# Scores and weighted sums in halves, and the work of every step in a new order on all engines

## What is computed

```python
def attn_layer(x, Wqkv, qs, ksc, Wo):
    qkv = x @ Wqkv
    q, k, v = jnp.split(qkv, 3, -1)          # 16 heads of 64
    q = l2norm(q) * qs
    k = l2norm(k) * ksc
    q = q * cos * scale + rotate_half(q) * sin * scale
    k = k * cos * inv + rotate_half(k) * sin * inv
    out = local_attention(q, k, v)           # softmax over this window and the one before
    return out @ Wo

def ffn_layer(x, g, bln, W1, b1, W2, b2):
    xn = (x - mu) / jnp.sqrt(var + 1e-05) * g + bln
    hg = xn @ W1 + b1
    a, gate = jnp.split(hg, 2, -1)           # 341 each
    return a * jax.nn.gelu(gate, approximate=False) @ W2 + b2

for i in range(6):
    x = attn_layer(shift_tokens(x), ...) + x
    x = ffn_layer(shift_tokens(x), ...) + x
```

## Time and profile before

| | |
|---|---|
| median of 3 runs | 1618.8 us (1618.2 to 1619.11) |
| the profiled execution, its own time | 1619.38 us |
| its span in the profile | 1617.6 us |
| TensorE busy | 1544.3 us, 95% |
| weight loads | 907.8 us, 56% |
| VectorE, ScalarE, GpSimd busy | 1234.8, 1232.5, 1222.1 us, each 76% |
| instructions of TensorE | 30224 MATMUL and 30224 LDWEIGHTS |
| mean granted clock | 0.987 |

### The profile page before, as it was taken

How to read it: one execution, slowest core, us unless ns; L and a number is a source line. 1 busy time by engine, 2 the same in 40 slices (tenths; PEclk the granted TensorE clock), 3 DMA queues, 4 the chain that set the end, 5 groups by cost and what they waited for, 6 DMA issues and landing times.

```text
span 1617.6 us, 69676 instructions
## 1 busy us (share of the span) xinstructions
PE 1544.3 (95%) x30224; PEld 907.8 (56%) x30224; DVE 1234.8 (76%) x1693; ACT 1232.5 (76%) x2368; POOL 1222.1 (76%) x1051
## 2 busy tenths in 40 slices
PE   7879999999999999999999999999999999999995
PEld 6745556555555555555556555555565565555553
DVE  5488878778778778777877778778778788787873
ACT  4347787787787787887887887887887887887871
POOL 6169888777787778778777787787787787787861
PEclk9989999999999999999999999999999999999998
DMA  5000000100000100000100000100000000000000
GB/s 193 28 2 27 10 7 5 61 7 6 22 6 7 35 29 10 18 7 9 36 28 10 9 16 10 33 31 9 9 16 9 7 5 9 7 18 9 7 12 27
DMA packets 24545, 32.60 MB, mean 20 GB/s; under 512 B 2372, under 2 KB 21424, under 8 KB 23344
## 3 DMA queue, kind: packets, MB, share of 16 engines
q1 hardware_dynamic: 24240, 28.15, 5.4%
HBM read 20.80 MB, written 1.05 MB: 14 GB/s over the span
## 4 chain that ended last, share of the span: by engine, by line
PE 75%; ACT 7%; issue 5%; DVE 3%; POOL 1%; DMA 0%; ACTq 0%; SPq 0%; POOLq 0%; DVEq 0%
PE ring L274 20%; PE psq L254 18%; PE ring L262 9%; PE ring L308 8%; PE pss L292 7%; PE ring L325 4%; PE ring L318 4%; PE pss L283 2%; DVE qb L927 2%; ACT L1126 2%; ACT sq L1096 1%; ACT uT L1126 1%; ACT pr L1100 1%; ACT kT L1107 1%; PE ring L649 1%
## 5 line engine op out<-in xcount | busy, mean ns | idle before, releaser
L254 PE MATMUL psq<-wqk,x0S 128*128 128x512 f32 x768 | 379.4, 617 | 4.0 <-issue 3.1
L274 PE MATMUL ring<-mh,x0S 128*32 128x512 f32 x3072 | 369.6, 598 | 7.4 <-ACT uT L1126 7.4
L1305 POOL TENSOR_TENSOR qa<-qa,qb 128x1024 f32<-128x1024 f32 x96 | 228.9, 2384 | 63.0 <-DVE qb L848 62.9
L1361 POOL TENSOR_TENSOR pr<-pr,rden 128x1024 f32<-128x1024 f32 x96 | 183.9, 1915 | 88.3 <-DVE rden L824 88.0
L1357 POOL TENSOR_TENSOR qa<-qa,qb 128x1024 f32<-128x1024 f32 x96 | 226.7, 2361 | 0.4 <-DVE qb L927 0.3
L254 PEld LDWEIGHTS psq<-wqk,x0S 128*128 128x128 f32 x768 | 135.8, 192 | 130.0 <-issue 120.8
L308 PEld LDWEIGHTS ring<-u,pT 128*32 128x32 f32 x6144 | 172.9, 111 | 61.4 <-issue 61.4
L904 DVE TENSOR_TENSOR qa<-psq,tab 128x1024 f32<-128x1024 f32 x96 | 117.5, 1224 | 105.5 <-PE psq L254 105.5
L308 PE MATMUL ring<-u,pT 128*32 128x128 f32 x6144 | 187.0, 274 | 3.2 <-ACT pT L1228 3.2
L1323 POOL TENSOR_TENSOR qa<-qa,rn 128x1024 f32<-128x1024 f32 x96 | 182.7, 1903 | 7.5
L274 PEld LDWEIGHTS ring<-mh,x0S 128*32 128x32 f32 x3072 | 80.0, 109 | 190.5 <-issue 172.6
(11 more groups left out here) (174 smaller groups left out, 2819.8 us busy)
## 6 DMA issues: line engine op xcount, KB each, us to landing
wqk<-in_wqk SPq DMA_DIRECT2D x6, 1024.0 KB, 4.9
mvT<-in_mvT SPq DMA_DIRECT2D x6, 512.0 KB, 5.6
wo<-in_wo SPq DMA_DIRECT2D x6, 512.0 KB, 8.7
xf<-x SPq DMA_DIRECT2D x24, 128.0 KB
xf<-x SPq DMA_DIRECT2D x24, 127.0 KB
rope<-in_rope SPq DMA_DIRECT2D x1, 2048.0 KB, 10.0
w<-in_w SPq DMA_DIRECT2D x6, 341.0 KB, 3.8
xmid<-in_x SPq DMA_DIRECT2D x4, 256.0 KB, 4.0
```

Of the source, the lines that this page charges most:

```text
L254: return mm(psq[:, 512 * (n % 2):512 * (n % 2) + 512], x0S[:, tile * P:tile * P + P], wqk[:, l % 2, 512 * n:512 * n + 512], start=True, st ...
L274: last = mm(bank[WIN * g:WIN * g + WIN, :], x0S[:, tile * P + WIN * w:tile * P + WIN * w + WIN], mh[:, l % 2, g, :, :].rearrange("p j n -> ...
L1305: g_.tensor_tensor(qa[:, t % 2, 0:1024], qa[:, t % 2, 0:1024], qb[:, 0:1024], ALU.add).then_inc(sum_q, 1)
L1361: g_.tensor_tensor(p4[t % 2], p4[t % 2], rden[:, :].unsqueeze(1).unsqueeze(3).broadcast_to([P, 2, HEADS, WIN]), ALU.mult).then_inc(p_ready, 1)
```

## The change

Four edits of TensorE's work go together, with a new order and new lags on every engine:

- `scores` is called twice a tile, pairs 0 to 3 after the mask at the end of step t+3, pairs 4 to 7 in step t+4. `mix` is called twice, and the values of U0 stand between its halves.
- `project` and `hidden` get a second form, in pieces of 32 columns, which no call uses: `WHOLE_P` and `WHOLE_H` list every product as whole.
- The lags: keys and queries of tile t in step t+1, both transposes one behind the other in t+3, P in t+5, Y in t+6 (five steps behind the projections; before, three). F stands 12 steps behind the projection of its group's first tile (before, 8), Z 14 (before, 11), X 15 (before, 12). TensorE's step is now the step of the other engines, and the loop has two steps more.
- The scan's chunks 4 to 7 stand in step 0, ahead of the first projection; 8 to 11 in step 1, 12 to 15 in step 2.
- ACT, DVE and POOL are put in the matching order; the semaphores `l_bst` and `l_rs` are split in two; weight loads of the feed-forward part are issued two steps later (`LOAD_W` 9).

```diff
+WHOLE_P = [0, 1, 2, 3]
+WHOLE_H = [(0, 1), (1, 1), (2, 1), (0, 0), (1, 0), (2, 0)]
...
-            def scores(t):
-
-                for pair in range(PAIRS):
+            def scores(t, half):
+
+                for pair in range(4 * half, 4 * half + 4):
...
-            def mix(bank, t):
-
-                for b in range(4):
+            def mix(bank, t, part):
+
+                for b in (2 * part, 2 * part + 1):
...
-            for s in range(STEPS + 17):
...
+            for s in range(STEPS + 19):
...
+                t = s - 4
+                if 0 <= t < STEPS:
+                    scores(t, 1).then_inc(s_ready, 1)
...
+                    mix(ring[bank], t, 0)
...
+                    values(ring[bank], t, 0).then_inc(filled[bank], 1)
...
+                    mix(ring[bank], t, 1).then_inc(filled[bank], 1)
...
+                t = s - 3
+                if 0 <= t < STEPS:
+                    wait(pe, p_shifted, t)
+                    mask(t)
...
+                    scores(t, 0)
```

More of the change, by code:

```diff
@@ L498, in _ @@
             features(0)
-            for s in range(STEPS + 17):
-                t = s - 7
+            for s in range(STEPS + 19):
+                t = s - 6
                 if 0 <= t < STEPS:
-                    bank, n = take("U2", t)
-                    wait(pe, freed[bank], n)
-                    values(ring[bank], t, 2).then_inc(filled[bank], 1)
                     bank, n = take("U3", t)
@@ L525, in _ @@
[L525 to L534, removed]
+                u = unit_at(s, 3)
+                if u >= 0:
+                    features(u)
@@ new lines, in _ @@
+                i = group_at(s, 14)
+                if i >= 0:
+                    bank, n = take("G0", i)
+                    nbank, m = place["F", i]
+                    pe.wait_ge(freed[nbank], m + 1)
+                    if i % GROUPS == 0:
+                        pe.wait_ge(w1_ready, 16 * (i // GROUPS + 1))
+                    wait(pe, freed[bank], n)
+                    hidden(ring[bank], 0, 1).then_inc(filled[bank], 1)
+                    bank, n = take("A0", i)
+                    wait(pe, freed[bank], n)
+                    hidden(ring[bank], 0, 0).then_inc(filled[bank], 1)
@@ new lines, in _ @@
+                i = group_at(s, 15)
+                if i >= 0:
+                    bank, n = take("A1", i)
+                    wait(pe, freed[bank], n)
+                    hidden(ring[bank], 1, 0).then_inc(filled[bank], 1)
+                    bank, n = take("A2", i)
+                    wait(pe, freed[bank], n)
+                    hidden(ring[bank], 2, 0).then_inc(filled[bank], 1)
+                t = s - 5
+                if 0 <= t < STEPS:
+                    bank, n = take("U1", t)
+                    wait(pe, freed[bank], n)
+                    values(ring[bank], t, 1).then_inc(filled[bank], 1)
@@ new lines, in _ @@
+                if i >= 0:
+                    act.wait_ge(nmr_ready, i + 1)
+                    if i > 0:
+                        abank, m = place["A2", i - 1]
+                        act.wait_ge(filled[abank], m + 1)
+                    for k in range(QUAD):
+                        last = nc.scalar.activation(xh[:, k * P:k * P + P].rearrange("p (a n) -> p a n", a=2), xf[:, :, k, :],
+                                                    ACT.Identity, bias=nmr[:, k:k + 1], scale=rstd[:, k:k + 1])
+                    last.then_inc(xh_ready, 1)
```

712 lines of the change are left out of this document (344 added, 368 removed).

## The result

| | median, us | runs | profiled run: span |
| --- | --- | --- | --- |
| before | 1618.95 | 1618.2 to 1619.3 | 1617.6 |
| changed | 1636.3 | 1631.97 to 1637.26 | 1635.5 |

The change makes the kernel slower: the ratio is 1.0103, 95% interval [1.0084, 1.0121]. The prediction said 1612 us, with 1602 to 1627 as its range.

What follows compares the result with a forecast made beforehand. TensorE bounds the middle, other engines' latency the ends. Work +19.2, Gelu wait -8.5, `issue` waits -13.5, head +3 and tail -7 sum to -6.8 us: 1612 us, range 1602 to 1627.

Steps and rivals of the forecast that it cites:

- (a) to (g): TensorE's own work in the steady part: added and joined runs of one shape, +0.80 us a group, +19.2 us in all.
- (b): Scores cut into two runs: 0.73 us a half against 1.39 us whole, +0.07 us a tile.
- rival 4: Each half of the scores starts on a full queue, 0.70 us, and the head costs nothing: 1603 us; chance 0.14.
- (h): TensorE's values no longer wait for a ring bank behind the Gelu of L1126: 0.37 us, 23 times, -8.5 us.
- (i): Spreading TensorE's burst of 304 instructions in 2.26 us ends nearly all waits for `issue`: -13.5 us.
- New waits: Steady part: the tight loop over `psq` keeps a 0.4 us margin and no ring bank is late: 0 us.
- Rival 1: The loop over `psq` is late, 0.25 us 96 times, +24 us: 1636 us; chance 0.10.
- The ends: Head +3 us (-4 to +9) from a later first projection; tail -7 us (-12 to +3) from a shorter wait for Z.
- the -7: Tail: more tiles under way fill TensorE's wait for Z, so the last Y comes some 7 us earlier.

Runs made afterwards that it cites:

- experiment 10: The kernel before with G1 and A0 in swapped order on TensorE: 1611.6 us, ratio 0.9953.
- experiment 6: The kernel before with the scores in two halves, the second behind the keys' projection, ahead of U0: 1625.8 us, ratio 1.0031.
- experiment 9: The kernel before with mask and whole scores moved behind the keys' projection, ahead of U0: 1643.0 us, ratio 1.0156.
- experiment 12: The kernel before with the second half of the scores behind the keys' projection and G1 and A0 swapped: 1617.2 us, ratio 0.9991.
- experiment 1: The changed kernel with the second half of the scores directly behind the first, so one run again: 1677.2 us, ratio 1.0348.
- Kernel 2: The changed kernel with U1 ahead of the hidden products, so G0, A0 and A1, A2 cut no values: 1622.6 us, ratio 1.0014.
- experiment 4: The changed kernel with the scan's chunks in the loop one step later on all engines: 1636.7 us, ratio 1.0099.
- experiment 3: The changed kernel with the transposes F and X ahead of the queries' projection: 1640.1 us, ratio 1.0115.
- experiment 7: Kernel 2 with F and X moved right behind the queries' projection, ACT's work on both ahead of the probabilities: 1626.6 us, ratio 1.0040.
- experiment 8: The kernel of experiment 7 with G1 and G2 behind the queries' projection too: 1640.0 us, ratio 1.0111.
- kernel 5: The kernel before with the scores in two halves, the second right behind the transposes of the probabilities: 1628.5 us, ratio 1.0050.

## Why the prediction was wrong, step by step

**(a) to (g), TensorE's own work: +19.2 predicted, +27 measured.** Four steps without `merge` took 60.55 us before, 0.38 of it the wait behind the Gelu, and take 61.29 now: +1.12 us of work a group, not +0.80, and 24 of them. By terms: the joined transposes -0.14 a tile, as said; U0 within `mix` 0 (2.742 against 2.743 us), as said; hidden products between values +0.33 a pair, said 0.34; G1 and G2 on their own within 0.01 of it; Z -0.20, as said; F and X +0.15 and +0.19 instead of 0.20. Each rule that was read from a row with the whole run in it held to 0.05 us. The Trainium skill ("TensorEngine Tiling (Array Packing)", Key Properties) says that a change of the tiling mode drains TensorE. The trace agrees in so far as each run that begins anew costs 0.13 to 0.20 us beyond its streams.

**(b), the halves, is the first step that failed.** The prediction took 62 of the 128 MATMULs, started 0.585 us after the first, for a half, and put an exit behind it. A half has 64, and its end isn't like the middle of a whole: its last eight MATMULs start from 0.534 to 0.627 us, where the same eight of a whole run start from 0.534 to 0.585; the whole has its slow eight too, at its own end. So a half is 0.627 + 0.146 = 0.77 us, and behind the transposes it begins 0.016 us later still. +0.17 instead of +0.07 a tile is +9.5 us. The row was the right one, but it shows the middle of a run, and a cut makes a new end. The upper bound of the term, +0.20, would have been nearer: it is the run cost of every other shape. The Trainium skill ("TensorE: Matmul & The Clock Gate", the table at its top) gives TensorE a queue of 64 instructions. A gain from a filled queue, which rival 4 put at 0.70 us a half, didn't show: the halves take 0.77 and 0.79 us.

**(h), the wait behind the Gelu: -8.5 predicted.** It is gone, and experiment 10 shows its worth by itself: -8.0 us.

**(i), the waits for `issue`: -13.5 predicted.** They fell from 11.8 us (12.1 in the whole run) to 2.5 us between 150 and 1540 us. With the loss behind them (above the medians of the same MATMULs) it was 13.6 us before and is some 4 to 6 now, depending on how much of what isn't shown as idle is counted: -8 to -10. The mechanism is shown (experiments 6, 9 and 12), the size was 3.5 to 5.5 us too large, and the way to count, the densest 2.3 us, was wrong.

**New waits: 0 predicted.** Behind 221 us that held, by a hair, as experiment 1 showed. Rival 1, which named 1636 us, did not come about there: that its time is nearly the measured one is chance. The waits for ACT's squares, 9.8 us in seven (the kernel before had 0.7 us in two), all lie ahead of 221 us.

**The ends, -4 predicted, about +8 measured, are the second step that failed.** The total rose by 17.9 us in the profiled runs; +27 for work, -8.9 for the Gelu and -8 to -10 for `issue` leave some +8 to +10. Kernel 2, with the same ends, gives nearly as much: +3.0 in all, of which +10.9 is work (60.62 - 60.17 = 0.45 us a group), -8.9 and -6.3 are waits, which leaves +7.3. The first weighted sum starts at 162.76 us, not at 134.49; the last MATMUL of all the sums starts 36.3 us before the end, not 35.1. Between the first and the last the changed kernel takes 11.5 us less, for the work of two more tiles lies ahead of the first. The steps ahead of the first:

```profile
140.76 1.98 PE L251 MATMUL psq<-wqk,x0S 128*128 128x512 f32 x4 [1.24 <-ACT sq L1146]
...
146.42 1.96 PE L251 MATMUL psq<-wqk,x0S 128*128 128x512 f32 x4 [1.10 <-ACT sq L1245]
...
152.65 1.99 PE L251 MATMUL psq<-wqk,x0S 128*128 128x512 f32 x4 [1.35 <-ACT sq L1146]
```

A step without `mix` and with few values is too short to hide the loop over `psq`, and each half of it costs a wait of 1.1 to 1.35 us: these steps take 12.4 to 12.5 us from keys to keys. The prediction saw that two more steps stand there ("after six projections, not four"), but charged only the later start of the first projection, 6 us, and took most of that back. In experiment 4 a first projection 8.5 us earlier brought nothing. At the other end TensorE's wait for Z fell from 9.01 to 4.70 us, as said:

```profile
1611.03 5.49 PE L332 MATMUL ring<-w,uT 128*128 128x128 f32 x24 [4.70 <-DVE uT L840]
```

That is the 4 to 5 us of the -7. But the last sum stands no nearer to the end for it.

The waits can't be the whole of the ends. Over the whole run TensorE's idle time fell from 73.3 to 58.6 us and its busy time rose from 1544.3 to 1576.9 us, by 32.6 where the work rose by 27. One reason stands in the windows: between 76 and 150 us the granted clock was 0.73, not 0.84, so that TensorE stood at the lower of its two levels (1.2 GHz) for some 40 us of the 74 instead of 24; at that level the first projection of the earlier trace rows takes 3.62 us instead of 1.98. In the last stretch it was 0.93, not 0.89. The two new waits for `issue` in the scan's chunks, 2.6 us, belong to the ends as well. Which end loses depends on where one looks: counted by the keys' projections, the sixth starts at 158.9 us instead of 161.8, and it is the part from the last one's start to the end, with two more tiles on their way, that grew, from 77.2 to 91.5 us. No run of its own tried how much of the rest is due to the depth of the pipeline, how much to the order within a step and how much to the clock. That the ends cost 7 to 10 us is what the measured terms leave; that the two further steps cause it is argued from these rows and stays open.

**The chances.** The errors of (b), +9.5, (i), at least +3.5, and the ends, about +12, all point the same way and make some 25 us; the other terms of the work were off by 1.7 us the other way. The range had its upper bound for (b) at 0.20 a tile, but took the ends and (b) each at its middle and let only one fail at a time.

## What to carry to other kernels

Cutting a run of small products costs as much as any other change of shape, 0.17 us here, whatever the middle of the run suggests: price a cut by a row in which such a run ends, and multiply by the tiles before anything else. A wait for a bank is better mended by changing the order in which two products take their banks (8 us here, for nothing) than by a new order of everything. And spreading instructions pays only where it is free: look at what a product hides before it is moved. In experiment 1 a half of the scores had given ACT its time; in experiments 3, 7 and 8 slow products behind fast ones seem to have given the fetch its time.

## What the runs showed of the hardware

- A late instruction inside a run of the values costs 0.4 to 1.0 us more than the idle time that the trace shows (kernels 1, 3, 7, 8, 9), inside `mix` 0.2 to 0.4 (kernel 9), as I read it because two of a set of four go alone and the later sets are shifted. In the scores the wait of the earlier trace rows cost 1.92 us for 1.71 shown, against the median of the same MATMUL.
- The waits for `issue` hang on the place in the program, not on the time: in the kernel before and in kernels 5 and 10 they fall at the same MATMULs (numbers 5644, 10448, 15252 and 23089 of 30224), though those start at 326 to 1222, 329 to 1228 and 324 to 1214 us. 304 instructions in 2.3 us gave 16 waits, 416 in 4.4 us gave 34, 272 in 3.5 us none. Which size of packet or buffer makes this so was not tried.
- F adds 0.44 us behind a projection and ahead of the values (kernel before), 0.49 behind one and ahead of transposes (kernel 7), 0.51 ahead of one (kernel 3), and 0.59 as a run between the scores and the values (changed kernel).
